# TensorE's order in an attention step: both pairs of scores moved against the matmuls that make row maxima

## What is computed

```python
xn = layernorm(x)                                  # x: 2 x 1024 x 128, float32
# differential attention, 16 sub-heads of width 8, 8 value heads of width 16
q, k = rope(xn @ Wq.T) * 8**-0.5, rope(xn @ Wk.T);  v = xn @ Wv.T
probs = softmax(q @ k.T)                           # per sub-head, 1024 x 1024
attn = (probs[even] - lam * probs[odd]) @ v        # per head
attn = attn * rsqrt(mean(attn**2) + 1e-5) * (1 - LAMBDA_INIT)
# mixture of zones: a router picks 3 of 8 zones per batch element
ffn = xn + sum_e w[b, e] * gelu(xn @ Wa[e]) @ Wb[e]
return x + attn @ Wo.T + ffn
```

## Time and profile before

| | |
|---|---|
| median of 3 runs | 475.67 us (475.26 to 476.3) |
| the profiled execution | 473.91 us, span in the trace 472.1 us |
| granted TensorE clock, mean | 0.967 |
| busy, share of the span | PE 92%, DVE 82%, ACT 70%, PEld 41%, POOL 28% |
| exps, 256 | 245.9 us busy |
| maxima on VectorE, 512 | 319.5 us busy |
| chain that ended last | PE 60%, ACT 10%, issue 9%, DVE 8% |

### The profile page before, as it was taken

How to read it: one execution, slowest core, us unless ns; L and a number is a source line. 1 busy time by engine, 2 the same in 40 slices (tenths; PEclk the granted TensorE clock), 3 DMA queues, 4 the chain that set the end, 5 groups by cost and what they waited for, 6 DMA issues and landing times.

```text
span 472.1 us, 7272 instructions
## 1 busy us (share of the span) xinstructions
PE 432.7 (92%) x2623; PEld 192.8 (41%) x2623; DVE 385.4 (82%) x726; ACT 332.2 (70%) x430; POOL 131.9 (28%) x154
## 2 busy tenths in 40 slices
PE   7396599999999899999999999999999999999987
PEld 6385355666666423323333333333333333322235
DVE  2788278999898969998999999999999998986225
ACT  1431255555555478889888988898889888989972
POOL 4157699978686400000001001000001000000000
PEclk9597799999999979999999999999999999999999
DMA  8507863200000040002000201000000000000002
GB/s 308 205 1 237 314 258 120 95 28 20 3 1 1 6 175 1 2 2 91 3 1 1 91 25 67 3 1 1 2 3 1 3 1 1 1 2 3 1 0 90
DMA packets 12038, 25.65 MB, mean 54 GB/s; under 512 B 1250, under 2 KB 5986, under 8 KB 11874
## 3 DMA queue, kind: packets, MB, share of 16 engines
q1 hardware_dynamic: 11570, 22.37, 13.6%
q10 hardware_dynamic: 432, 2.81, 1.6%
HBM read 15.48 MB, written 9.44 MB: 53 GB/s over the span
## 4 chain that ended last, share of the span: by engine, by line
PE 60%; ACT 10%; issue 9%; DVE 8%; POOL 5%; DMA 4%; SPq 2%; ACTq 0%; POOLq 0%
PE ps L1019 19%; PE ps L989 16%; PE ps L1012 10%; ACT E L573 8%; DVE part_max L734 6%; PE ps L952 3%; DMA X<-in_x 3%; POOL hL L440 2%; PE ps L870 2%; PE ps L953 2%; PE ps L954 2%; PE ps L872 2%; PE ps L871 2%; POOL rope L406 1%; DMA q_scr<-ropeL 1%
## 5 line engine op out<-in xcount | busy, mean ns | idle before, releaser
L734 DVE TENSOR_REDUCE part_max<-ps 128x1 f32<-128x512 f32 x512 | 319.5, 681 | 37.0 <-PE ps L989 33.6
L573 ACT ACTIVATE E<-ps 128x1024 f32<-128x1024 f32 x256 | 245.9, 1027 | 38.0 <-PE ps L1012 37.2
L1019 PE MATMUL ps<-E,Vg 128*32 128x512 f32 x1024 | 138.1, 612 | 1.2 <-ACT E L573 1.1
L989 PE MATMUL ps<-K,Q 32*128 32x512 f32 x384 | 110.8, 477 | 3.3 <-DVE part_max L734 2.8
L1012 PE MATMUL ps<-Q,K 32*128 32x512 f32 x384 | 88.9, 485 | 7.0 <-ACT E L573 5.3
L989 PEld LDWEIGHTS ps<-K,Q 32*128 32x128 f32 x384 | 46.6, 184 | 93.3 <-DVE part_max L734 89.4
L440 POOL TENSOR_TENSOR hL<-h,hH 128x512 fp32r<-128x512 f32 x48 | 61.4, 1288 | 12.3 <-ACT hH L545 11.6
L543 ACT ACTIVATE h<-ps 128x512 f32<-128x512 f32 x48 | 28.6, 597 | 38.2 <-PE ps L872 24.9
L1012 PEld LDWEIGHTS ps<-Q,K 32*128 32x128 f32 x384 | 36.2, 184 | 37.3 <-ACT E L573 33.2
L478 POOL TENSOR_TENSOR U<-AT,rsum 128x256 f32<-128x256 f32 x15 | 9.3, 621 | 145.1 <-DVE rsum L789 136.3
L431 POOL CAST neg_max<-neg_f 128x16 fp32r<-128x16 f32 x16 | 3.1, 197 | 118.0 <-DVE neg_f L743 118.0
(11 more groups left out here) (148 smaller groups left out, 418.3 us busy)
## 6 DMA issues: line engine op xcount, KB each, us to landing
k_scr<-ropeH SPq DMA_DIRECT2D x6, 512.0 KB, 5.0
K<-k_scr SPq DMA_DIRECT2D x6, 512.0 KB, 4.5
Q<-q_scr SPq DMA_DIRECT2D x6, 512.0 KB, 5.8
tab<-in_tables ACTq DMA_DIRECT2D x1, 2048.0 KB, 11.2
q_scr<-ropeL SPq DMA_DIRECT2D x4, 512.0 KB, 5.6
q_scr<-ropeH SPq DMA_DIRECT2D x4, 512.0 KB, 6.7
wa_raw<-in_wa SPq DMA_DIRECT2D x6, 256.0 KB, 2.8
wb_raw<-in_wb SPq DMA_DIRECT2D x6, 256.0 KB, 3.2
```

The source lines that it names most:

```text
L573: nc.scalar.activation(E[:, par, 2 * jj:2 * jj + 2, :].rearrange("p j t -> p (j t)"), ps[:, 2 * jj:2 * jj + 2, :].rearrange("p j t -> p (j ...
L734: nc.vector.tensor_reduce(part_max[:, tile // FC % 2, j * FC + tile % FC, sh:sh + 1], ps[:, SLOT_BANK[quad_slot(t) + k], :], AX.X, ALU.max ...
L989: mm(ps[:, SLOT_BANK[x], :], Qs[g % KQ_BUFS][strip(j), tile % TB * P:(tile % TB + 1) * P], Ks[g % KQ_BUFS][strip(j), sh * BANK:(sh + 1) * ...
L1019: last = mm(ps[QUAD * j:QUAD * (j + 1), B_PV, :], Vg[:, par, st, j // 2, :], E[:, s % 2, k, :], start=(st == 0), stop=(st == TB - 1), skip ...
```

## The change

Of the two pairs of scores, the first pair of step s+2 is now made at the end of loop step s, behind the products with V, and three maxima stand in one piece ahead of the second pair. The first pair of step 1 is made ahead of the loop. Waits move with what they guard.

```diff
+            pe.wait_ge(exp_done, 1)
+            score(1, 0)
+            score(1, 1)
             for s in range(ALL_STEPS):
                 nxt = s + 1
                 made = max_slots(s)
-                for t, k in made[:1]:
-                    max_slot(t, k)
-                if nxt < ALL_STEPS:
-                    if nxt % TB == 0:
-                        pe.wait_ge(qmax_in, 32 * (nxt // TB + 1))
-                    pe.wait_ge(exp_done, 2 * s + 1)
-                    score(nxt, 0)
-                    score(nxt, 1)
-                for t, k in made[1:2]:
+                for t, k in made[:3]:
                     max_slot(t, k)
                 if nxt < ALL_STEPS:
                     pe.wait_ge(exp_done, 2 * s + 2)
                     score(nxt, 2)
                     score(nxt, 3)
-                for t, k in made[2:]:
+                for t, k in made[3:]:
                     max_slot(t, k)
...
                 pe.wait_ge(exp_done, 2 * s + 2)
                 probs_v(s % STEPS, s // STEPS % 2)
+                if nxt + 1 < ALL_STEPS:
+                    if (nxt + 1) % TB == 0:
+                        pe.wait_ge(qmax_in, 32 * ((nxt + 1) // TB + 1))
+                    pe.wait_ge(exp_done, 2 * nxt + 1)
+                    score(nxt + 1, 0)
+                    score(nxt + 1, 1)
```

## The result

The changed kernel takes 480.06 us (median of 4 runs, 479.28 to 481.2) against 475.47 us for the kernel before on the same chip: ratio 1.0121, 95% interval 1.0099 to 1.0143, so it is slower by 1.2%. Forecast were 479.0 us, or +3.3; measured are +4.6.

What follows compares the result with a forecast made beforehand. Bound: a ring of dependencies through TensorE's order, no engine full. Terms -2.1 + 3.3 + 2.0 = +3.2 us, on the median 475.67 + 3.3 = 479.0 us; range 471.0 to 483.0.

Steps and rivals of the forecast that it cites:

- What bounds the loop: Attention loop, steps 1 to 115: no engine is full; a ring of dependencies through TensorE's order sets 2.27 us a step.
- Point 1: The 87 steps of three maxima without transpose: first pair no longer held, most gain comes back; 183.0 to 180.9, -2.1 us.
- The ceiling of 10 us: Most that steps of three could save through the loop of exp, second pair, products, first pair: 48 x 0.42 / 2.
- Point 2: The 17 steps of four maxima without transpose: 2.92 us where the first maximum is in strip 0 or 2; +3.3 us.
- Point 3: The 11 steps with the transpose of maxima: +0.57 us each in steps 28, 38 and 48; sum +2.0 us.
- The bound for a held first maximum: Its read was taken 0.42 us after its start; carried, not held gives -3.4 us, a read at 0.53 gives +7.0.
- Rival A: The loop through ScalarE decides: the 10 us come in full, costs stay at 5.3; -4.7, 471.0 us; chance 0.24.
- Rival B: Strict order on TensorE: a held matmul holds those behind it; -1.2, 474.5 us; chance 0.08.
- Rival C: Held first maxima are read later, at 0.53, and VectorE starves; +7.0, 482.7 us; chance 0.12.
- D: No change: steps of three and with transpose cancel steps of four, if first maxima are rarely held; chance 0.08.
- the signs named ahead: In the trace: three-slot steps 1.7 to 2.5 us, TensorE's second pair released by part_max, steps 116 to 127 unchanged, among others.
- the chain of 2.70: Length of a step of four set by the ring of three banks: 1.00 + 0.53 + 0.68 + 0.06 + 0.43 us.

Runs made afterwards that it cites:

- short reads: VectorE reads each maximum over half of its tile only: 462.89 us in the order before, 458.12 us in the changed order.
- other strips: Strips of the maxima chosen anew from quad 36 on to avoid those of neighbouring scores: changed order 470.59 us, order before 466.19 us.
- the worst strips: Changed kernel with strips chosen the wrong way round, first maximum in a strip of the first pair: 492.05 us.

## Why the prediction was right, point by point

The sum of +3.2 us for the steps (+3.3 on the median) came out as +4.45. All three of its terms have the right sign and are within 0.6 us of the trace, so the number was not luck.

- **What bounds the loop** held: a ring of dependencies in TensorE's list. The rules for starts and banks were taken from a few steps of the trace. The eight expectations worked out from them all give the loop's difference with its right sign and within 1.0 us of the trace.
- **Point 1, steps of three**: -1.81 against -2.1. That a large gain stands behind it and comes back through late banks was argued there. The short reads show it, with 9.9 us when a read takes 0.27 less. The ceiling of 10 us counted 48 steps with a first maximum in strip 0 or 2; of the 87 steps it is 45, which makes 9.5.
- **Point 2, steps of four**: +3.67 against +3.3. The ten whose first maximum is held brought 2.4 of that (forecast 2.2): nine take 2.92 to 2.94, one 3.06; forecast were 2.92. The other seven brought 1.3 (forecast 1.1), but not for the reason given: the second pair holds no maximum in any of the seventeen, since the fourth starts 0.48 us or more behind that pair. The prediction had them at 2.70, and none of them is there. What they show instead is below.
- **Point 3, the transpose**: +2.59 against +2.0. Steps 28, 38 and 48 rose by 1.82 together, forecast were 3 times 0.57 = 1.71; step 48 took 3.22 against the 3.24 that was worked out. Undoing the placement in these three brought 1.28 back. The eight others rose by 0.8, forecast were 0.3 at most (2.0 less 1.71).
- **The sum was 1.2 us too small**, and the term that was mis-sized is the read of a first maximum that is *not* held. It was taken as 0.53 after the start of its matmul, as where the first maximum leads. Now two scores start just ahead of it. Timeline of step 47, whose products before it start at 275.80:

```profile
276.80 0.50 PE L1012 MATMUL ps<-xnH 32*128 32x512 f32 x2
276.80 0.85 PE L989 MATMUL ps<-xnL 32*128 32x512 f32 x3
...
277.40 3.84 DVE L734 TENSOR_REDUCE part_max<-ps 128x1 f32<-128x512 f32 x6 [0.29 <-PE ps L989]
```

  The read starts 277.40 - 276.80 = 0.60 after it. From 176 to 431 us the changed kernel has 21 such reads for which VectorE stands idle, all at 0.59 to 0.60, and the kernel before has 59 at 0.53 to 0.54. 21 times 0.06 is 1.3 us, an estimate of the most that the term can bring, against 1.2 missing.

  Steps of four show it singly: of the seven whose first maximum is not held, three take 2.76 or 2.77, which is 1.00 + 0.59 + 0.68 + 0.06 + 0.43. In the other four (2.81 to 3.15) VectorE is still busy when the first tile is ready, with reads left from the step before and, in steps 17, 75 and 98, with its work for the output (`query_rows`).

  The same term fits the two expectations that the other strips missed. In the changed order 50 reads with VectorE idle start at 0.59 to 0.60, which can cost 50 times 0.06 = 3.0 us at most. The order before was expected 1 to 2 us ahead without this term, and is 2.7 ahead from step 4 on. No run took the term away by itself, so its share in the sums is an estimate.
- **The bound for a held first maximum** (0.42, between not held and 0.53) was well chosen: its 40 reads in the changed kernel with VectorE idle start at 0.42 to 0.43.
- **Rival A** (the loop through ScalarE decides, faster) is what happens when reads are short: there steps of three gain 9.9 us and the others lose 4.6, close to its 10 and 5.3. With full reads it does not happen. **Rival B** (strict order in the queue) gave -1.2, measured was +4.6, and it had the order before at 265.6 us. That is 5.6 us above the 260.0 of the other rules and 4.0 above the trace (the prediction says 5.7 above the trace). The Trainium skill, "TensorE: Matmul & The Clock Gate", section "The mechanism", says what rival B goes by: matmuls start and end strictly in program order. The trace does not agree with that for matmuls in different strips of rows: in the earlier trace rows the maximum at 276.20 starts before the score at 276.45 that stands ahead of it in the program. **Rival C** asked for reads of held maxima at 1.86; they are at 1.77. **D** (no change) fell with the interval.
- Of the signs named ahead three more did not show as they were told. Steps of three take 1.66 to 3.03 us, seven of them above 2.5, though their mean is lower by 0.02 as told. Steps 116 to 127 take 0.22 us longer. And TensorE's second pair is not booked as waiting for part_max: the wait stands at the third maximum ahead of it, and the pair follows by a few ns.

Not tried: a fourth bank for the ring, which would test the chain of 2.70 itself. PSUM has none free.

## What to carry to other kernels

In a list that several engines wait for, price a move by what stands behind each wait, and by which resources neighbours share (here a strip of rows), not by the number of instructions. An order that is right for the score loop can be wrong as long as banks come back late: look for a shorter read, or another choice of strips, before reordering. Here the choice of which sub-head goes into which slot, with the same work, brought 1.6%, while the new order cost 1.2%.

## What the runs showed of the hardware that was not expected

- A matmul that starts as the third within 10 ns, each in another strip, is read 0.59 to 0.60 us after its start. One that starts as the first is read after 0.53 (283.01 to 283.54). Whether its place or the two scores ahead of it make the difference was not separated.
- A matmul held by its strip starts 0.33 after the one that is in it (294.59 to 294.92 in the kernel with the worst strips), and those behind it in other strips go ahead of it.
